# A router's logits and low-rank rows computed with tokens on the partitions: one sandwich layer on one core

## What is computed

```python
logits = jnp.einsum('bsd,ed->bse', x, gate_W) + gate_b            # 8 experts
top1 = jnp.argmax(jax.nn.softmax(logits, axis=-1), axis=-1)
base = jnp.einsum('bsd,fd->bsf', x, wi_W) + wi_b                  # 1024 wide
for i in range(8):
    lora = jnp.einsum('bsr,fr->bsf', jnp.einsum('bsd,rd->bsr', x, lora_A[i]), lora_B[i])   # rank 4
    inter = jax.nn.relu(base + lora)
    expert_out = jnp.einsum('bsf,df->bsd', inter, wo_W) + wo_b
    out = out + (top1 == i)[..., None] * expert_out
```

## Time and profile before

| | |
|---|---|
| median of 3 runs | 535.78 us (535.15 to 537.13) |
| profiled execution, first to last instruction | 533.86 us; its own device time is not listed |
| busy: PE / DVE / ACT / POOL | 509.3 / 467.3 / 454.1 / 344.7 us |
| granted TensorE clock, mean | 0.994 of full speed |
| start of one steady batch to the next | 58.97 us |

### The profile page before, as it was taken

How to read it: one execution, slowest core, us unless ns; L and a number is a source line. 1 busy time by engine, 2 the same in 40 slices (tenths; PEclk the granted TensorE clock), 3 DMA queues, 4 the chain that set the end, 5 groups by cost and what they waited for, 6 DMA issues and landing times.

```text
span 533.9 us, 8929 instructions
## 1 busy us (share of the span) xinstructions
PE 509.3 (95%) x2752; PEld 412.8 (77%) x2752; DVE 467.3 (88%) x1005; ACT 454.1 (85%) x1238; POOL 344.7 (65%) x544
## 2 busy tenths in 40 slices
PE   8899989899999999999999999999999999899995
PEld 6666645688897779877897779877887778677995
DVE  5599999987999999998999899989999899995554
ACT  3499988999899998999899998999899989895320
POOL 5697037415991798539991798449981969597272
PEclk9989999999999999999999999999999999999998
DMA  7694353016230535026230635035400660310011
GB/s 233 194 239 112 95 143 80 1 34 170 63 89 1 146 93 152 6 68 170 50 111 1 160 79 158 1 100 137 111 9 16 174 163 5 80 41 1 1 40 41
DMA packets 22691, 47.63 MB, mean 89 GB/s; under 512 B 5266, under 2 KB 13586, under 8 KB 22004
## 3 DMA queue, kind: packets, MB, share of 16 engines
q1 hardware_dynamic: 21956, 45.95, 32.5%
q0 software_dynamic: 256, 0.52, 0.4%
q10 hardware_dynamic: 432, 0.59, 0.3%
HBM read 8.24 MB, written 4.19 MB: 23 GB/s over the span
## 4 chain that ended last, share of the span: by engine, by line
PE 52%; ACT 30%; POOL 6%; SPq 4%; DVE 3%; issue 2%; DMA 1%; POOLq 0%; ACTq 0%
PE pu L199 25%; ACT ps L523 22%; PE ps L227 10%; PE pu L283 5%; SPq L1202 3%; ACT y L590 3%; PE pu L239 3%; PE ps L199 2%; PE ps L206 2%; POOL y L1032 2%; DMA stack<-qk 1%; POOL nmr L1026 1%; PE pu L305 1%; ACT qk L537 1%; POOL xb L1038 1%
## 5 line engine op out<-in xcount | busy, mean ns | idle before, releaser
L523 ACT ACTIVATE ps<-ps,nmax 128x512 f32<-128x512 f32 x512 | 346.2, 705 | 19.8 <-DVE nmax L735 19.6
L735 DVE TENSOR_REDUCE nmax<-ps 128x1 f32<-128x512 f32 x512 | 324.5, 681 | 25.9 <-PE ps L227 24.3
L227 PE MATMUL ps<-stack 128*128 128x512 f32 x512 | 186.7, 420 | 2.3 <-ACT ps L523 1.6
L523 ACT ACTIVATION_READ_ACCUMULATOR ps<-ps,nmax 128x1 f32 x512 | 129.4, 253 | 0.0
L227 PEld LDWEIGHTS ps<-stack 128*128 128x128 f32 x512 | 93.5, 190 | 27.1 <-ACT ps L523 12.5
L199 PEld LDWEIGHTS pu<-wo_r,inter 128*128 128x128 f32 x744 | 95.4, 188 | 3.8
L199 PE MATMUL pu<-wo_r,inter 128*128 128x256 f32 x744 | 97.2, 282 | 0.0
L199 PE MATMUL pu<-yT,wi_r 128*128 128x512 f32 x336 | 87.4, 395 | 0.0
L199 PEld LDWEIGHTS pu<-yT,wi_r 128*128 128x128 f32 x336 | 63.2, 188 | 14.0 <-ACT xn L590 0.2
L206 PE MATMUL ps<-ones_r 128*128 128x512 f32 x132 | 55.1, 459 | 7.7 <-ACT ps L523 6.5
L1046 POOL TENSOR_TENSOR ml<-gs,g 128x128 f32<-128x128 f32 (+1 forms) x9 | 3.5, 387 | 77.9 <-DVE g L887 77.9
(11 more groups left out here) (157 smaller groups left out, 673.5 us busy)
## 6 DMA issues: line engine op xcount, KB each, us to landing
stack<-qk SPq DMA_DIRECT2D x256, 128.0 KB, 2.5
xb<-in_x SPq DMA_DIRECT2D x7, 512.0 KB, 3.5
out_y<-xb SPq DMA_DIRECT2D x7, 512.0 KB, 3.5
xb<-in_wo SPq DMA_DIRECT2D x1, 1024.0 KB, 7.9
vo<-in_wi SPq DMA_DIRECT2D x2, 512.0 KB, 6.8
oT<-in_wqk ACTq DMA_DIRECT2D x1, 512.0 KB, 4.2
xb<-in_x SPq DMA_DIRECT2D x4, 128.0 KB, 4.2
stack<-qk SPq DMA_DIRECT2D x8, 64.0 KB, 2.5
```

Source lines behind the costliest of these rows:

```text
L227: e.matmul(ps[i % NS][:], st[:, 1 - p, c, t * 128:(t + 1) * 128], st[:, 2, c, :], start=True, stop=True).then_inc(scored, 1)
L523: e.activation(ps[i % NS][:], ps[i % NS][:], ACT.Exp, bias=nmax[:, i % 8:i % 8 + 1], accum_out=ssum[:, b % 2, t, h:h + 1]).then_inc(exped, 1)
L735: e.tensor_reduce(nmax[:, i % 8:i % 8 + 1], ps[i % NS][:], AX_X, ALU.max, negate=True).then_inc(maxed, 1)
```

## The change

`gates` swaps the operands. The tokens are now stationary, 128 at a time, and the gate's 80 (or 40) columns are streamed, so for four token tiles there are 16 matmuls and the result has tokens on the partitions: 4 x 80 columns in one bank. `gate_t`, `fold`, `gT` and ACT's `gate` and `logits` are gone. DVE's `gate_1` adds the high and low products straight out of PSUM into `gs` (a reduce over 2) and then adds the bias, which is now a 128x8 tile, to the logits. The bank of the gate is let go by `logits_here`, which DVE now signals. On DVE `gate_1` stays at its place, and on PE `gate` does.

```diff
-            def gates(out_, yt):
-                e.matmul(out_[0:80], wg_r[:, 0, :], yt(0, 0), start=True, stop=False)
-                e.matmul(out_[0:40], wg_r[:, 0, 0:40], yt(1, 0), start=False, stop=False)
-                e.matmul(out_[0:40], wg_r[:, 1, 0:40], yt(1, 1), start=False, stop=False)
-                return e.matmul(out_[0:80], wg_r[:, 1, :], yt(0, 1), start=False, stop=True)
+            def gates(bank, yt, ts):
+                for i, t in enumerate(ts):
+                    o, tok = bank[:, i * 80:(i + 1) * 80], slice(t * 128, (t + 1) * 128)
+                    e.matmul(o, yt[:, 0, 0, tok], wg_r[:, 0, :], start=True, stop=False)
+                    e.matmul(o[:, 0:40], yt[:, 1, 0, tok], wg_r[:, 0, 0:40], start=False, stop=False)
+                    e.matmul(o[:, 0:40], yt[:, 1, 1, tok], wg_r[:, 1, 0:40], start=False, stop=False)
+                    p = e.matmul(o, yt[:, 0, 1, tok], wg_r[:, 1, :], start=False, stop=True)
+                return p
...
-                    bank = banks[take(("gate", b), gT_here, b + 1)]
+                    bank = banks[take(("gate", b), logits_here, b + 1)]
                     e.wait_ge(yT_low, 2 * b + 2)
-                    gates(bank, lambda a, c: yT[:, a, c, :]).then_inc(gate_ps, 1)
-
-            def gate_t(b):
-                if here(b):
-                    bank = banks[take(("gs", b), logits_here, b + 1)]
-                    e.wait_ge(gT_here, b + 1)
-                    for t in range(NT):
-                        p = e.matmul(bank[:, t * 40:(t + 1) * 40], gT[:, t * 128:(t + 1) * 128], fold[:], start=True, stop=True)
-                    p.then_inc(gs_ps, 1)
+                    gates(bank, yT, ALL).then_inc(gate_ps, 1)
...
-                slot(34), q_k(b + 1, 1), slot(35), gate_t(b - 1)
+                slot(34), q_k(b + 1, 1), slot(35)
...
-                slot(34), q_k(b + 1, 2), gate(b - 1), slot(35)
-                slot(36), q_k(b + 1, 1), logits(b - 1), slot(37)
+                slot(34), q_k(b + 1, 2), slot(35)
+                slot(36), q_k(b + 1, 1), slot(37)
...
-                    n = GATE_STEPS * (b + h)
+                    n, nt = GATE_STEPS * (b + h), ts.stop - ts.start
                     lg = gs[:, ts, 0:8]
+                    bank = bank_of[("gate", b) if b < B - 1 else ("gate", b, h)]
+                    if b == 0:
+                        e.wait_ge(bg_loaded, 16)
+                    else:
+                        e.wait_ge(masked, MASK_STEPS * b)
+                    e.wait_ge(gate_ps, b + h + 1)
+                    e.tensor_reduce(gs[:, ts, :], bank[:, 0:80 * nt].rearrange("p (t a m) -> p t m a", t=nt, a=2), AX_X,
+                                    ALU.add).then_inc(logits_here, 1)
                     e.wait_ge(logits_here, b + h + 1)
+                    e.tensor_tensor(lg, lg, bg_s[:].unsqueeze(1).to_broadcast([128, nt, E]), ALU.add).then_inc(gated, 1)
+                    e.wait_ge(gated, n + 1)
                     e.tensor_reduce(g1[:, 0, ts], lg, AX_X, ALU.max).then_inc(gated, 1)
```

More of the change, by code:

```diff
@@ L24 @@
 NS = 5
-GATE_STEPS, MASK_STEPS = 10, 4
-CONSTS, LATE = 11, 23
+GATE_STEPS, MASK_STEPS = 11, 4
+CONSTS, LATE = 11, 22
 ALL, HALVES = (0, 1, 2, 3), ((0, 1), (2, 3))
@@ L68, in sandwich @@
         wg_s = sb("wg_s", [128, 2, 40])
-        bg_s = sb("bg_s", [80, 1])
-        fold = sb("fold", [80, 40])
+        bg_s = sb("bg_s", [128, E])
         id_s = sb("id_s", [128, 128])
@@ L120, in sandwich @@
         xnT_ps, qk_ps, v_ps, oT_ps, y_ps, yT_ps = (sem(n + "_ps") for n in ("xnT", "qk", "v", "oT", "y", "yT"))
-        gate_ps, gs_ps, lt_ps, f1_ps, f2_ps = (sem(n + "_ps") for n in ("gate", "gs", "lt", "f1", "f2"))
+        gate_ps, lt_ps, f1_ps, f2_ps = (sem(n + "_ps") for n in ("gate", "lt", "f1", "f2"))
         xnT_high, qk_high, yT_high, f1_high = (sem(n + "_high") for n in ("xnT", "qk", "yT", "f1"))
@@ L128, in sandwich @@
         f1_last_high, f1_last_low = sem("f1_last_high"), sem("f1_last_low")
-        v_here, oT_here, y_here, gT_here, lt_here, y2_here = (sem(n + "_here") for n in ("v", "oT", "y", "gT", "lt", "y2"))
+        v_here, oT_here, y_here, lt_here, y2_here = (sem(n + "_here") for n in ("v", "oT", "y", "lt", "y2"))
         f2_tile_ps, y2_tile_here, tile_stored = sem("f2_tile_ps"), sem("y2_tile_here"), sem("tile_stored")
@@ L362, in gate_half @@
                 b = B - 1
-                bank = banks[take(("gate", b, h), gT_here, b + h + 1)]
+                bank = banks[take(("gate", b, h), logits_here, b + h + 1)]
                 e.wait_ge(yT_low, 2 * b + h + 1)
-                gates(bank[:, 0:256], lambda a, c: yT_last[:, a, c, cols(h)]).then_inc(gate_ps, 1)
-            def gate_t_half(h):
-                b = B - 1
-                bank = banks[take(("gs", b, h), logits_here, b + h + 1)]
-                e.wait_ge(gT_here, b + h + 1)
-                for t in HALVES[h]:
-                    n = 40 * (t % 2)
-                    p = e.matmul(bank[:, n:n + 40], gT[:, t * 128:(t + 1) * 128], fold[:], start=True, stop=True)
-                p.then_inc(gs_ps, 1)
+                gates(bank, yT_last, HALVES[h]).then_inc(gate_ps, 1)
             def masked_t_half(h):
@@ L489, in tensor @@
             slot(28), slot(29), gate(b - 1)
-            slot(30), gate_t(b - 1), slot(31)
+            slot(30), slot(31)
             slot(32), f2(b - 2, 3, 1), slot(33)
@@ L556, in y_t @@
                     e.activation(yT[:, 0, c], bank_of["yT", b, c][:], ACT.Copy).then_inc(yT_high, 1)
-            def gate(b):
-                if here(b):
-                    e.wait_ge(gate_ps, b + 1)
-                    e.activation(gT, bank_of["gate", b][0:80, :], ACT.Identity, bias=bg_s[:, 0:1]).then_inc(gT_here, 1)
-            def logits(b):
-                if here(b):
-                    e.wait_ge(gs_ps, b + 1)
-                    if b:
-                        e.wait_ge(masked, MASK_STEPS * b)
-                    e.activation(flat(gs[:]), bank_of["gs", b][:, 0:160], ACT.Copy).then_inc(logits_here, 1)
             def gate_exp(b):
                 if here(b):
-                    e.wait_ge(gated, GATE_STEPS * b + 2)
+                    e.wait_ge(gated, GATE_STEPS * b + 3)
                     e.activation(g8[:, 1], g8[:, 0], ACT.Exp).then_inc(gate_exped, 1)
@@ L600, in y_half @@
                 e.activation(yT_last[:, 0, :, cols(h)], parts(bank_of["yT", b, h]), ACT.Copy).then_inc(yT_high, 1)
-            def gate_half(h):
-                b = B - 1
-                e.wait_ge(gate_ps, b + h + 1)
-                e.activation(gT[:, cols(h)], bank_of["gate", b, h][0:80, 0:256], ACT.Identity,
-                             bias=bg_s[:, 0:1]).then_inc(gT_here, 1)
-            def logits_half(h):
-                b = B - 1
-                e.wait_ge(gs_ps, b + h + 1)
-                e.wait_ge(masked, MASK_STEPS * b)
-                e.activation(flat(gs[:, 2 * h:2 * h + 2, :]), bank_of["gs", b, h][:, 0:80],
-                             ACT.Copy).then_inc(logits_here, 1)
             def gate_exp_half(h):
                 ts = slice(2 * h, 2 * h + 2)
-                e.wait_ge(gated, GATE_STEPS * (B - 1 + h) + 2)
+                e.wait_ge(gated, GATE_STEPS * (B - 1 + h) + 3)
                 e.activation(g8[:, 1, ts], g8[:, 0, ts], ACT.Exp).then_inc(gate_exped, 1)
@@ L707, in scalar @@
             slot(28), slot(29)
-            slot(30), gate(b - 1), slot(31), logits(b - 1)
+            slot(30), slot(31)
             slot(32), gate_exp(b - 1), slot(33)
@@ L1155, in pool @@
             e.tensor_tensor(lb_r[32:64], lst[32:64], lb_r[32:64].bitcast(F32), ALU.subtract).then_inc(late, 1)
-            e.wait_ge(id_loaded, 16)
-            e.wait_ge(late, 22)
-            e.tensor_tensor(fold[:], id_s[0:80, 0:40], id_s[0:80, 40:80], ALU.add).then_inc(late, 1)
             e.wait_ge(late, LATE)
```

31 lines of the change are left out of this document (14 added, 17 removed).

## The result

The changed kernel takes **547.42 us** (median of 4 runs, 544.79 to 549.10) against 535.76 before, beside it: a ratio of 1.0208, 95% interval 1.017 to 1.0246. It is slower, as forecast, but by 11.7 us and not by 7.6; the median lies above the forecast range (537.8 to 546.0). Its four runs spread over 4.3 us, those of before over 2.0. The profiled execution is one of the two long ones, 549.07 us; the other two, 544.79 and 545.77, lie inside the forecast range.

What follows compares the result with a forecast made beforehand. No engine rests; each steady batch's chain runs on PE until 286 us, then on ACT. Steady batches 5.35, first gate 0.3, batch 6's gate 0.2 and tail 1.8 sum to 7.65 us: 535.78 becomes 543.4 us, range 537.8 to 546.0.

Steps and rivals of the forecast that it cites:

- Steady batches: Batches b = 2 to 6: gate_exp and all behind it on ACT late, 1.07 us each, 5.35 us in all.
- hand-over from PE to ACT: Steady batch at 286 us: the chain passes from PE to ACT; delaying ACT's exponentials after it delays the next batch equally.
- VectorE: DVE's gate_1: the added sum takes 0.48 us and the bias 0.19, with gaps 0.73 us together.
- Matmul pace: PE's gate: 16 matmuls at 0.118 us each take 1.89 us, 0.97 more than the four before.
- disagrees: On the skill page's faster path for 128-column loads: the trace's f32r load lies on the narrower loads' line, contradicting it.
- The waits: Steady batch: ACT waits about 1.5 us for q_k(b+1, 1) and about 0.8 us at gate_exp for DVE.
- Tail: After the last batch: project(7, 2) waits for its bank, f2 stops midway, half fold gone; 1.8 us longer.
- Gate of batch 6: In the last batch: old waits go, but 16 matmuls hold back score 34; gate_exp 0.2 us later.
- First gate: Gate at b = 1, among filler matmuls: later waits take up most of ACT's delay; 0.3 us.
- Loads hide: Rival on PE's gate: the 16 matmuls cost only 0.5 to 0.9 us; 2.3 us slower, 538.1 us; chance 12%.
- ScalarE was the bound: Rival on steady batches: ACT's 1.07 us less per batch all comes back; 532.2 us; chance 8%.
- Full price: Rival on PE's gate: short f32r matmuls at 0.23 us each, 2.76 extra per gate; 18 us slower, 554; chance 4%.

Runs made afterwards that it cites:

- e2_gate_late: Changed kernel with PE's 16 gate matmuls moved behind q_k(b+1, 1), where the fold stood, in loops 1 to 6: 543.13 us, ratio 1.0122 to before.
- e8_eight: Changed kernel with 8 gate matmuls for 16 (the low part of yT left out of the logits): 540.78 us, ratio 1.0095 to before.
- e6_late_both: Changed kernel with gate matmuls where the fold stood, gate_exp one slot later, shifted bank ring and ten filler matmuls in the last batch: 537.06 us, ratio 1.0022.
- e5_fillers: Changed kernel with the bank ring shifted at the tail and ten unread matmuls in PE's waits of the last batch: 543.13 us, ratio 1.0143 to before.
- e14_fill_only: Changed kernel, gate and banks unchanged, with ten unread matmuls in last-batch PE waits and five ahead of project(7, 2): 544.57 us, ratio 1.0158 to before.

## Why the prediction was right and wrong

**Right, by mechanism and size.** *Steady batches:* 5.38 us for 5.35, so close only because small errors cancel: the 16 matmuls took 0.77 us more than the four and not 0.97, and `gate_exp` came 1.01 later and not 1.09, but that batch was 1.11 longer (60.07 for 58.96), so some 0.1 was lost behind the gate, where the forecast put nearly nothing. The hand-over from PE to ACT was the place to read, and the price was set by what stands ahead of `q_k(b+1, 1)` on PE; e2_gate_late and e8_eight show it from two sides. *VectorE:* the sum took 0.478 us for 0.48, the bias 0.19. *Matmul pace:* 1.70 us for 16, inside the bounds of 1.66 and 1.93, under the 1.89 taken; the loads' line of the earlier trace rows was the better guide than the nearest row in kind. By the rule of the Trainium skill, "TensorE: Matmul & The Clock Gate", section "Weight-path perf modes — Fast Weight Load (FWL) and DoubleRow", as the prediction read it, these loads would have been quicker; the pace of 0.111 and the records of 192 ns show no faster path for f32r. That need not contradict the page: its table gives the path no win for fp32 and doesn't say what float32r counts as, so the prediction's "disagrees" was too strong. *The waits* were forecast as about 1.5 and 0.8 and are 1.21 and 0.68. *Tail:* both bank waits came where they were put, about 1.66 for 1.8. *Gate of batch 6:* 0.1 for 0.2.

**Wrong: the sum had no term for TensorE's clock.** The steps that failed are "The gate of batch 6 in the last batch" and "The tail", not in the length of their waits but in what follows them. The prediction counted the waits there once, at their own length, and took all durations behind them from rows at full clock. It also said of the gate of batch 6 that the waits go: the one of 0.63 us ahead of the fold went, but two new ones, 0.67 and 0.17, came right in front of the 0.75 and the 0.78 that had been there. In the profiled execution the clock fell behind these waits and again behind those of the tail, and half speed stood for 7 and 3.4 us where PE is on the chain: 4.4 us, with 0.87 more in loop b = 1. Its mean clock was 0.985; of the other three runs one had 0.981 and 549.10 us, the others 0.991 and 0.994, and 544.79 and 545.77 us. With the waits filled and nothing else changed the kernel takes 544.57, 1.2 from the forecast's 543.4 and inside its range. The risk could be seen in the trace before, where PE is busy 1.18 and 1.22 us of the two windows at 460 to 464 us. That the clock would fall could not, since there it did not; and it doesn't fall in every run, so on which side of the range's end a median of four came out was in part chance.

**Small misses.** *First gate:* 0.56 for 0.3; why is not shown, but ACT waits 1.44 and 0.65 us at that gate, more than the cover of the earlier trace rows takes up. *Range:* it rested on prices of instructions only; a spread of 4.3 us between runs of one kernel had no place in it.

**The rivals.** *Loads hide* fell with the pace of 0.111. *ScalarE was the bound* fell too: in e6_late_both PE's gate is out of the way, ACT has its 1.07 us less, and the batch is as long as before. But ACT still waits 0.31 and 0.37 us for DVE there, and no run got both waits to nothing, so what ACT's shorter queue would be worth without them is not shown. *Full price* (0.23 each) is excluded.

## What to carry to other kernels

Where work moves in a queue, price it by what stands directly behind it on the chain: the same 16 matmuls cost 1.07 us a batch ahead of `q_k(b+1, 1)` and nothing behind it. When an operation takes fewer turns in a ring of buffers, follow the ring to the program's end; two waits of the tail came from that alone, and one line mended them. Where PE has several waits close together, count them twice, as waits and as a chance of half speed behind them. A few idle matmuls that fit into the waits are a cheap insurance: ten cost nothing in e5_fillers, while the five of e14_fill_only that were longer than their wait cost 0.29 us.
